# Five later loads issued further back in the queue, a semaphore for each half of the queries, and fillers moved in two layer heads

## What is computed

```python
x = x + tanh(g_xattn[l]) * xattn_l(layernorm(x), ctx, ...)   # 16 heads of depth 8, 77 keys
x = x + tanh(g_ffn[l])   * ffn_l(layernorm(x), ...)
```

## Time and profile before

| | |
|---|---|
| median of 3 executions | 768.7 us (764.02 to 770.03) |
| the profiled execution | 768.5 us, span 766.6 us, so 1.9 us lie around the span |
| mean granted TensorE clock | 0.915 |
| busy share | PE 81%, DVE 68%, ACT 45%, POOL 36% |
| layer 0 (attention and its feed-forward stage) | 0 to some 210 us |
| head of layer 2, head of layer 3 | some 368 to 377 us, 507 to 514 us |
| the experts | from some 590 us to the end |

### The profile page before, as it was taken

How to read it: one execution, slowest core, us unless ns; L and a number is a source line. 1 busy time by engine, 2 the same in 40 slices (tenths; PEclk the granted TensorE clock), 3 DMA queues, 4 the chain that set the end, 5 groups by cost and what they waited for, 6 DMA issues and landing times.

```text
span 766.6 us, 10146 instructions
## 1 busy us (share of the span) xinstructions
PE 621.0 (81%) x3004; PEld 383.9 (50%) x3004; DVE 518.6 (68%) x1362; ACT 343.5 (45%) x654; POOL 279.0 (36%) x554
## 2 busy tenths in 40 slices
PE   5776878466899999898798882488788999998997
PEld 3433434244665564564444431243344776776885
DVE  8685545889863563387736648864557989879664
ACT  3142565355434344254263440316454665564553
POOL 5333354311350412116440730330222457535463
PEclk9797998799999999799899995589988999999999
DMA  8855322002214323002354330225300333433332
GB/s 259 203 154 156 91 64 57 1 0 69 70 39 139 95 33 90 10 1 83 124 152 150 58 86 0 68 74 145 110 5 0 112 108 107 132 95 94 110 123 66
DMA packets 67991, 67.73 MB, mean 88 GB/s; under 512 B 25120, under 2 KB 48224, under 8 KB 67553
## 3 DMA queue, kind: packets, MB, share of 16 engines
q1 hardware_dynamic: 61326, 64.61, 30.2%
q10 hardware_dynamic: 6610, 2.47, 1.3%
HBM read 50.29 MB, written 17.60 MB: 89 GB/s over the span
## 4 chain that ended last, share of the span: by engine, by line
PE 40%; DVE 20%; POOL 11%; issue 11%; DMA 11%; ACT 4%; SPq 4%; POOLq 0%; DVEq 0%; ACTq 0%
POOL sg L733 8%; PE ps L1872 7%; PE ps L1852 5%; PE ps L1812 5%; DMA QG<-q_parts 4%; DVE mraw L1424 3%; DMA q_parts<-loT 2%; PE ps L1774 2%; PE ps L2051 2%; PE ps L2042 2%; PE ps L1791 1%; PE ps L1757 1%; PE ps L1856 1%; PE ps L1855 1%; PE ps L1763 1%
## 5 line engine op out<-in xcount | busy, mean ns | idle before, releaser
L835 ACT ACTIVATE PT<-ps 110x512 f32<-110x512 f32 x192 | 111.4, 595 | 136.9 <-PE ps L1852 66.3
L1424 DVE TENSOR_REDUCE mraw<-ps 128x4 f32<-128x308 f32 x256 | 116.0, 476 | 67.7 <-PE ps L1812 26.8
L1812 PE MATMUL ps<-KG,QG 98*128 98x308 f32 x256 | 106.0, 433 | 38.6 <-DVE mraw L1424 23.1
L733 POOL TENSOR_TENSOR sg<-sg,cb 128x512 f32<-128x512 f32 x64 | 85.4, 1335 | 73.9 <-ACT sg L1025 73.8
L1852 PE MATMUL ps<-QG,KG 128*110 128x512 f32 x192 | 91.5, 493 | 8.2 <-ACT PT L835 6.2
L1812 PEld LDWEIGHTS ps<-KG,QG 98*128 98x128 f32 x256 | 51.5, 205 | 79.4 <-DVE mraw L1424 56.1
L1872 PE MATMUL ps<-PT,VN 128*18 128x512 f32 x512 | 72.4, 639 | 0.0
L1662 DVE TENSOR_TENSOR ps<-ps,sg 128x512 f32<-128x512 f32 x72 | 50.3, 698 | 32.3 <-POOL sg L733 26.6
L597 POOL TENSOR_TENSOR nt<-nhv,rs 128x4 f32<-128x4 f32 (+1 forms) x78 | 18.1, 233 | 146.5 <-DVE rs L1146 132.1
L1852 PEld LDWEIGHTS ps<-QG,KG 128*110 128x110 f32 x192 | 34.1, 180 | 51.0 <-ACT PT L835 37.7
L1025 ACT ACTIVATE sg<-ps 128x512 f32<-128x512 f32 x72 | 43.0, 597 | 36.1 <-PE ps L2114 35.7
(11 more groups left out here) (315 smaller groups left out, 1435.5 us busy)
## 6 DMA issues: line engine op xcount, KB each, us to landing
cb<-c_parts SPq DMA_DIRECT2D x64, 256.0 KB, 3.2
QG<-q_parts SPq DMA_DIRECT2D x48, 256.0 KB, 3.8
KG<-k_parts SPq DMA_DIRECT2D x48, 154.0 KB, 3.1
q_parts<-hiT SPq DMA_DIRECT2D x14, 256.0 KB, 2.0
q_parts<-loT SPq DMA_DIRECT2D x14, 256.0 KB, 2.0
k_parts<-kmH SPq DMA_DIRECT2D x16, 154.0 KB, 2.4
k_parts<-kmL SPq DMA_DIRECT2D x16, 154.0 KB, 2.8
VN<-v_parts SPq DMA_DIRECT2D x16, 144.0 KB, 2.5
```

Source lines behind the costliest of these rows:

```text
L733: pool.tensor_tensor(sg[:, n % 3, :], sg[:, n % 3, :], cb[:, k % CRING, :], ALU.mult).then_inc(sc_done, 1)
L835: act.activation(PT[0:w, q % PTR, :], ps[0:w, 4 + q % 2, :], ACT.Exp, scale=SCALE[l]).then_inc(exp_done, 1)
L1424: dve.tensor_reduce(mraw[:, n % 2, i, g * HG:(g + 1) * HG], ps[:, u % 2, 0:GK].rearrange("p (h k) -> p h k", k=K), AX_X, ALU.max).then_inc ...
L1812: ins = pe.matmul(o, QG[0:KS, n % 3, g, q], KG[0:KS, n % 3, g, :], start=True, stop=l not in (1, 2))
```

## The change

1. The five loads are taken out of their place before the first step and stand in `later_weights()`, which SP calls in layer 0 at `k == 1`, behind `maxima_in` of pair 2 and ahead of `keys_out` of pair 4.
2. `q_out` is replaced by `q_hi_out` and `q_lo_out`. The two reads of the high part are issued when the high part has landed, the third when the low part has. The writers of `hiT` and `loT` wait for their own half alone.
3. Layer 3's head has one filler behind each of its six score tiles where it had two. The heads of layers 2 and 3 have three new fillers ahead of the turn of the maxima and two behind it.

```diff
--- before.py
+++ after.py
@@ -250,7 +250,7 @@
         ld_x = [sem(f"ld_x{b}") for b in range(B)]
         ld_neg, neg_first, neg_in, ld_rows = sem("ld_neg"), sem("neg_first"), sem("neg_in"), sem("ld_rows")
         v_fill, v_out = [sem(f"v_fill{l}") for l in range(L)], [sem(f"v_out{l}") for l in range(L)]
-        q_out, k_out = [sem(f"q_out{r}") for r in range(2)], [sem(f"k_out{r}") for r in range(2)]
+        q_hi_out, q_lo_out, k_out = [[sem(f"{n}{r}") for r in range(2)] for n in ("q_hi_out", "q_lo_out", "k_out")]
         const_set, ones_set = sem("const_set"), sem("ones_set")
         dve_chain, act_chain, pool_chain = sem("dve_chain"), sem("act_chain"), sem("pool_chain")
         l2w_ready, kv_ps, k_hi, k_lo, v_evac = [sem(n) for n in (
@@ -408,13 +408,14 @@
             def queries_in(n):
                 if n >= 2:
                     sp.wait_ge(q_hi, n + 1)
-                    sp.dma_start(q_parts[n, 0], hiT[:, n % 2, :].bitcast(F32)).then_inc(q_out[n % 2], 16)
+                    sp.dma_start(q_parts[n, 0], hiT[:, n % 2, :].bitcast(F32)).then_inc(q_hi_out[n % 2], 16)
                     sp.wait_ge(q_lo, n + 1)
-                    sp.dma_start(q_parts[n, 1], loT[:, n % 2, :].bitcast(F32)).then_inc(q_out[n % 2], 16)
+                    sp.dma_start(q_parts[n, 1], loT[:, n % 2, :].bitcast(F32)).then_inc(q_lo_out[n % 2], 16)
                 if n >= 3:
                     sp.wait_ge(st_ps, NCH * (n - 2))
-                sp.wait_ge(q_out[n % 2], 32 * (n // 2 + 1))
                 for part in range(3):
+                    if part % 2 == 0:
+                        sp.wait_ge((q_hi_out, q_lo_out)[part // 2][n % 2], 16 * (n // 2 + 1))
                     sp.dma_start(QG[32 * part:32 * part + 32, n % 3, :, :].bitcast(F32),
                                  q_parts[n, part // 2].rearrange("(g r) q -> r g q", g=G)).then_inc(qg_in[n % 3], 16)
 
@@ -455,11 +456,12 @@
             keys_out(2)
             keys_in(2)
             values_in(2)
-            sp.dma_start(m3f[:, :, :], a["m3"].partition_broadcast(P)).then_inc(ld_const, 16)
-            sp.dma_start(repb[:, :], a["repb"]).then_inc(ld_const, 16)
-            sp.dma_start(w1s[:, :], a["w1"]).then_inc(ld_ffn1, 16)
-            sp.dma_start(w2s[:, :, :], a["w2"].rearrange("(c p) d -> p c d", p=P)).then_inc(ld_ffn1, 16)
-            sp.dma_start(w8[:, :], a["w8"]).then_inc(ld_ffn1, 16)
+            def later_weights():
+                sp.dma_start(m3f[:, :, :], a["m3"].partition_broadcast(P)).then_inc(ld_const, 16)
+                sp.dma_start(repb[:, :], a["repb"]).then_inc(ld_const, 16)
+                sp.dma_start(w1s[:, :], a["w1"]).then_inc(ld_ffn1, 16)
+                sp.dma_start(w2s[:, :, :], a["w2"].rearrange("(c p) d -> p c d", p=P)).then_inc(ld_ffn1, 16)
+                sp.dma_start(w8[:, :], a["w8"]).then_inc(ld_ffn1, 16)
             for l in range(L):
                 for k in range(-2, B):
                     if k + 2 < B and l * B + k + 2 >= 2:
@@ -468,6 +470,8 @@
                         next_mask((k + 3) // 2)
                     if 0 <= k + 1 < B and l * B + k + 1 > 0:
                         maxima_in(sp, l * B + k + 1, range(G))
+                    if l == 0 and k == 1:
+                        later_weights()
                     if l == 1 and k in (-1, 1):
                         next_mask(4 + (k + 1) // 2)
                     if l == 2 and k == -1:
@@ -793,7 +797,8 @@
             def input_high(b):
                 act.wait_ge(xT_ready, nT(7, b) + 1)
                 if b < 2:
-                    act.wait_ge(q_out[b], 16 * N)
+                    act.wait_ge(q_hi_out[b], 8 * N)
+                    act.wait_ge(q_lo_out[b], 8 * N)
                 act.activation(in_of(b)[0], xnT[:, b, :], ACT.Copy).then_inc(hi3_ready, 1)
 
             def router_out(ts, bank):
@@ -810,14 +815,14 @@
                     n = l * B + b
                     act.wait_ge(q_ps, n + 1)
                     if n >= 2:
-                        act.wait_ge(q_out[n % 2], 32 * (n // 2))
+                        act.wait_ge(q_hi_out[n % 2], 16 * (n // 2))
                     act.activation(hiT[:, n % 2, :], ps[:, q_bank(l, b), :], ACT.Identity, bias=bq[:, l:l + 1]).then_inc(q_hi, 1)
 
                 def parts_out(b):
                     act.wait_ge(q_hi, b + 1)
-                    act.dma_start(q_parts[b, 0], hiT[:, b, :].bitcast(F32)).then_inc(q_out[b], 16)
+                    act.dma_start(q_parts[b, 0], hiT[:, b, :].bitcast(F32)).then_inc(q_hi_out[b], 16)
                     act.wait_ge(q_lo, b + 1)
-                    act.dma_start(q_parts[b, 1], loT[:, b, :].bitcast(F32)).then_inc(q_out[b], 16)
+                    act.dma_start(q_parts[b, 1], loT[:, b, :].bitcast(F32)).then_inc(q_lo_out[b], 16)
 
                 def maxima_out(b):
                     n = l * B + b
@@ -1410,7 +1415,7 @@
                     n = l * B + b
                     dve.wait_ge(q_hi, n + 1)
                     if n >= 2:
-                        dve.wait_ge(q_out[n % 2], 32 * (n // 2))
+                        dve.wait_ge(q_lo_out[n % 2], 16 * (n // 2))
                     dve.scalar_tensor_tensor(out=loT[:, n % 2, :], in0=ps[:, q_bank(l, b), :], scalar=bq[:, l:l + 1],
                                              in1=hiT[:, n % 2, :].bitcast(F32), op0=ALU.add,
                                              op1=ALU.subtract).then_inc(q_lo, 1)
@@ -1902,7 +1907,7 @@
                         for b, u in units_of(l, k, c):
                             scores(b, u // G, u % G)
                             if k == -1 and l != 1:
-                                fill(2 if l == 3 else 1)
+                                fill(1)
                         if c == 2 and 0 <= k and k + 2 < B:
                             queries(k + 2)
                         if 0 <= k < B:
@@ -1919,7 +1924,11 @@
                             pe.wait_ge(am_w_part, 1)
                             pe.transpose(ps[:, 3, 0:P], am[:, 1:2].to_broadcast([P, P]), ident[:, :]).then_inc(am_w_ps, 1)
                         if c == 7 and 0 <= k + 1 < B:
+                            if k == -1 and l >= 2:
+                                fill(3)
                             turn_maxima(k + 1)
+                            if k == -1 and l >= 2:
+                                fill(2)
                         if c == 1 and k == B - 1 and l == 0:
                             turn_ffn_weights()
                         if c == 5 and k == B and l == 0:
```

## The result

The changed kernel takes 763.38 us in the median of 13 runs (759.91 to 765.21), the kernel before 767.8 us in 13 runs beside them: the ratio is 0.9942, with a 95% interval of 0.9919 to 0.9965. Timed again on another occasion it came to 0.9934 (0.9912 to 0.9956). So it is faster by 4 to 5 us, which is less than 1%. Its profiled execution took 762.71 us, with a span of 760.7 against 766.6.

What follows compares the result with a forecast made beforehand. No single engine was taken to set the time; PE holds 40% of the chain. From 768.5 us, -1.1 - 3.5 + 2.8 + 1.8 - 1.9 - 3.0 = -4.9 gave 763.6 us, range 758.5 to 769.5.

Steps and rivals of the forecast that it cites:

- Start: Start of layer 0: split signal lets PE's first tile of pair 0 start earlier, until POOL's cast is late; gain 1.1 us.
- Rival 4: Pairs 0, 8 and 14: early reads only share DMA engines with the low write, winning nothing; -2.8, 765.7 us; chance 0.13.
- Pair 2: Layer 0, pair 2: with the five loads away, PE's query wait goes and DVE is late next; gain 3.5 us.
- that work does not start earlier: Pair 2: DVE's other work, quantising layer 0's weights until 58.99, keeps its start, limiting the gain to 3.5 us.
- The loads' new place: SP between maxima of pairs 2 and 3: 2.45 us of issue plus 0.3 for the key write, together +2.8 us.
- most of the data has passed: Low key write goes out over 3 us after the first load, so the 807 KB cost it only 0.3 us.
- The clock behind the wait: Behind pair 3's maxima: after 4.5 us of idling, 4 us of PE pass at half clock; loss 1.8 us.
- Rival 2: All four stretches: the clock stays up everywhere, each near its better bound; -9.3, so 759.2 us; chance 0.22.
- Layer 2: Pair 8's earlier reads give 0.5 us, the head with fillers 1.4 until ACT's normalisations are late; together 1.9 us.
- Layer 3: Head's six tiles with one filler each go at DVE's pace, gain 2.5 us; pair 14's queries 0.5; together 3.0.
- Rival 3: Heads of layers 2 and 3: fillers too few, clock still falls to half; -2.2, so 766.3 us; chance 0.12.
- Rival 5: SP between maxima of pairs 2 and 3: loads wrongly placed, price 8.2 us; ends at +3.5, 772.0 us; chance 0.10.

## Why the prediction was right, and where it was not

The forecast was 763.6 us and the result 763.38; its mechanism, gains early and in the heads with part of them given back at pair 3, is what the trace shows. That the two numbers are 0.2 us apart is luck: terms were off by up to 1.7 us, some too large and some too small, and two executions of the changed kernel differ by 1.2. By its steps:

- **Start, 1.1 forecast.** Over the nine profiled executions with the split the first tile starts at 25.50 to 26.12 (mean 25.75), over the five without at 25.86 to 27.40 (mean 26.71): 1.0 us, and POOL's cast is late next, as said. The two ranges just overlap, so this rests on the means. Not foreseen: at the first tile of pair 1 the lead is 2.1 us in the mean (1.4 to 2.4). There is less half clock behind the start: over 26 to 34 us the granted clock is 0.66 to 1.00 with the split (mean 0.78) and 0.52 to 0.79 without (mean 0.63), and 0.15 of 8 us is 1.2 us, about the 1.1 that are left to explain. The term was too small by the clock's share. That share does not go with the length of the idling before the first tile (2.69 us and 4.40 in the two executions of the changed kernel), and what ends the half clock sooner was not tested. Rival 4, by which early reads win nothing, falls.
- **Pair 2, 3.5 forecast.** The wait for queries went (in the second execution to 1.48 us) and DVE became late, as said. The prediction let DVE's other work start earlier only by the start's 1.1 us ("about 59 less 1.1") and so had the first maximum 4.6 us earlier than in the earlier trace rows. It came 5.9 us earlier in the changed kernel and 5.1 in its second execution. This is DVE of the first in time:

```profile
56.32 0.42 DVE L1205 TENSOR_TENSOR att<-ps,rden 128x256 f32<-128x256 f32 x1
56.66 0.85 DVE L1429 TENSOR_REDUCE mraw<-ps 128x4 f32<-128x308 f32 x2
```

  DVE's other work ended at 56.7, which is 2.3 us before 58.99, and in the second execution at 57.5, 1.5 before: that is the start's lead of 2.4 and 1.7. With split and fillers but the loads in their old place it ended at 56.8, 2.2 before, with a lead of 2.2, so it is not the loads that moved it. The step "that work does not start earlier" holds apart from the start's lead; the miss here is the start's term carried on, and not another one. In the first execution the lead of 5.9 us at pair 2's third tile then shrank to 3.6 in the half-clock stretch behind and came back to 5.0, of which 4.6 were forecast; the prediction priced this stretch nowhere in its main line. In the second the lead stayed at 5.1. So a start term that was too small and a pair 2 term that was too large nearly cancelled in the first execution.
- **The loads' new place, 2.8 forecast, 3.5 and 4.5 measured** (3.0 by the means of SP's stretch, 22.2 us in the five profiles with the loads in it and 19.2 in the eight without). The 2.45 us of issue were 2.7; the 0.3 for the key write was too low, it took 1.1. As an account of the path that is nearly right. As a cause it is not: the kernel that hides the issues gains nothing that can be measured, since the value writes then come later. The step that failed is "most of the data has passed".
- **The clock behind the wait, 1.8 forecast, 1.9 and 2.1 measured.** The wait was 5.23 us and 6.14 instead of 4.5, the clock 0.50. Filled, it stays at 1.00. Rival 2 is wrong here and right in the heads.
- **Layer 2, 1.9 forecast.** Pair 8's first tile came 0.7 and 0.6 us earlier, but 0.4 of this was gone by its last tile, so the term of 0.5 was too high. The head gave 1.4 and 1.3, and the stretch from there to layer 3 1.0 more in one execution and 0.5 in the other, which the prediction did not have; from 460 to 500 us PE's clock there is 0.57 in both and 0.50 before. ACT's normalisations were late next as forecast, PE's turn coming behind this row of ACT:

```profile
374.28 1.65 ACT L772 ACTIVATE xn<-x,nsh,rs 128x128 f32<-128x128 f32 x4 [3.73 <-POOL nsh L630]
```

- **Layer 3, 3.0 forecast, 4.0 and 3.1 measured.** Six tiles in 2.9 us against 5.27 before; about 3 were forecast, at DVE's pace. Rival 3, fillers too few, is ruled out by both heads at 1.00.
- **Rival 5** had the right place. But its price of 8.2 us was not reached: 5.4 to 6.5 us were lost at pair 3 and behind it.

**What stays open.** The parts don't add. Alone they give 6.7, 3.5 and -0.7 us, 9.5 together; the change gives 4.4 to 5.1. By the intervals (each part is known to some 1.3 to 1.8 us) the gap of over 4 us looks like more than noise. A possible part of the reason: in the profile of the split alone layer 3's head was at 1.00 anyway, so the fillers' share may be counted twice. In the kernel with split and fillers but the old loads, pair 2's half-clock stretch came out longer (57 to 72 at 0.50, against 0.76 with the split alone), and the lead of 2.0 us turned into 0.5 us behind. Why the same wait of 5 to 6 us is followed by half-clock stretches of different length was not settled; one profile for each kernel can't say whether this is the kernel's or the execution's.

## What to carry to other kernels

Before bulk loads are moved behind a wait, look for the next place where the queue has slack for their bytes and not only for their issues: here it lay one batch further, and was worth 5 us. Take the price of such a place from several profiles, since one alone was 0.8 us off the mean here. After a wait has been shortened or moved, read the granted clock of the stretch behind it and the idle time ahead; twelve matmuls into a free bank in that idle time won about as much again (4.4 us). Edits that touch the same clock stretches must be timed together, since their separate gains do not add.

## What was not expected of the hardware

- Waits of little over 2 us were followed by half clock here. At pair 3's maxima the seven profiles with a wait of 2.15 to 3.02 us have a granted clock of 0.50 to 0.66 over the 4 us behind it (the split alone: 2.15 and 0.57; loads in the slack: 2.48 and 0.66), and the four with 5.2 to 6.1 us have 0.50. With 1.69 us it was 1.00, and with fillers up to 1.66 us before the tile it was 1.00 too.
- Starting earlier paid more than it moved: the first tile came 1.0 us earlier in the mean and the first tile of pair 1 2.1, with a granted clock of 0.78 against 0.63 between (means over 26 to 34 us).
- The issue of a DMA is not of fixed length: the second of six value writes kept SP for 3.15 us behind the loads, for 1.12 in the kernel before, and the later ones take 0.80 (all six: 7.52 instead of 5.48 us).
